# MLP chunks of a two-layer adapter network: the 256-column LoRA products placed one by one among the 512-column products

## The reference, cut to what matters

```python
def lora_add(base, inp, A, B):
    Ab = A[layer_idx][lora_indices]
    Bb = B[layer_idx][lora_indices]
    t = jnp.einsum('bri,bni->bnr', Ab, inp)
    return base + jnp.einsum('bor,bnr->bno', Bb, t) * SCALE
gate = lora_add(jnp.einsum('bnh,fh->bnf', x, W_gate), x, A_gate, B_gate)
up = lora_add(jnp.einsum('bnh,fh->bnf', x, W_up), x, A_up, B_up)
act = jax.nn.silu(gate) * up
down = lora_add(jnp.einsum('bnf,hf->bnh', act, W_down), act, A_down, B_down)
```

## Time and profile before

| | us |
|---|---|
| median of 3 runs | 700.91 (700.26 to 701.99) |
| the profiled execution's own time | 702.66 |
| its span, first to last instruction | 700.6 |
| TensorE matmul busy | 675.9 (96%) |
| VectorE, ScalarE, GpSimd busy | 313.4, 296.5, 340.0 |

### The profile page before, as it was taken

How to read it: one execution, slowest core, us unless ns; L and a number is a source line. 1 busy time by engine, 2 the same in 40 slices (tenths; PEclk the granted TensorE clock), 3 DMA queues, 4 the chain that set the end, 5 groups by cost and what they waited for, 6 DMA issues and landing times. The chain is left out here.

```text
span 700.6 us, 11139 instructions
## 1 busy us (share of the span) xinstructions
PE 675.9 (96%) x3353; PEld 561.6 (80%) x3353; DVE 313.4 (45%) x739; ACT 296.5 (42%) x642; POOL 340.0 (49%) x262
## 2 busy tenths in 40 slices
PE   4799989999999999999999999999999999999997
PEld 3578778887788888888888888888888888887775
DVE  3788567746521223731222562142373124234664
ACT  2776543334643343653333464343365343344210
POOL 0034400141787666487766578776648867400000
PEclk9999999999999999999999999999999999999999
DMA  8973561031354336254335245433424524200112
GB/s 322 349 265 136 196 225 61 15 98 47 109 165 145 111 114 240 79 168 155 111 109 172 63 142 167 138 112 120 155 80 154 166 85 137 85 0 1 61 67 113
DMA packets 32210, 91.80 MB, mean 131 GB/s; under 512 B 5312, under 2 KB 5440, under 8 KB 30624
## 3 DMA queue, kind: packets, MB, share of 16 engines
q1 hardware_dynamic: 21936, 61.05, 25.9%
q0 software_dynamic: 10080, 30.16, 12.9%
q10 hardware_dynamic: 144, 0.00, 0.0%
HBM read 81.23 MB, written 9.96 MB: 130 GB/s over the span
## 5 line engine op out<-in xcount | busy, mean ns | idle before, releaser
L570 POOL TENSOR_TENSOR gu_lo<-gu_raw,gu_hi 128x1024 fp32r<-128x1024 f32 x44 | 113.7, 2584 | 101.2 <-ACT gu_hi L646 100.2
L1263 DVE TENSOR_TENSOR act_f<-psU,silu 128x512 f32<-128x512 f32 x44 | 30.4, 692 | 187.7 <-ACT silu L819 95.8
L601 POOL DMA_INDIRECT ab<-in_ab,idx_tab x88 | 86.6, 984 | 20.7 <-issue 16.2
L819 ACT ACTIVATE silu<-psG 128x512 f32<-128x512 f32 x44 | 26.2, 597 | 153.0 <-issue 89.1
L1380 PE MATMUL psD<-act_hi,dn_hi 128*128 128x512 f32 x176 | 69.0, 392 | 0.0
L1381 PE MATMUL psD<-act_lo,dn_hi 128*128 128x512 f32 x176 | 69.0, 392 | 0.0
L1382 PE MATMUL psD<-act_hi,dn_lo 128*128 128x512 f32 x176 | 68.6, 390 | 0.0
L570 POOL TENSOR_TENSOR dn_lo<-dn_raw,dn_hi 128x512 fp32r<-128x512 f32 x44 | 57.3, 1303 | 21.0 <-ACT dn_hi L646 20.9
L575 POOL DMA_INDIRECT h_scratch<-h,idx_s x22 | 23.7, 1077 | 64.1 <-ACT h L675 32.7
L1380 PE MATMUL psG<-x_hi,gu_hi 128*128 128x512 f32 x132 | 54.2, 411 | 0.6 <-ACT silu L819 0.6
L1382 PE MATMUL psG<-x_hi,gu_lo 128*128 128x512 f32 x132 | 51.7, 392 | 0.0
(11 more groups left out here) (346 smaller groups left out, 1706.4 us busy)
## 6 DMA issues: line engine op xcount, KB each, us to landing
gu_raw<-in_gu SPq DMA_DIRECT2D x44, 512.0 KB
dn_raw<-in_dn SPq DMA_DIRECT2D x44, 256.0 KB
cond_w_raw<-in_cond_w SPq DMA_DIRECT2D x8, 1024.0 KB, 7.3
x_all<-in_x_t SPq DMA_DIRECT2D x4, 1024.0 KB, 10.7
tok<-h_scratch SPq DMA_DIRECT2D x4, 1024.0 KB, 5.5
out_t<-x_all SPq DMA_DIRECT2D x16, 256.0 KB, 2.1
ab<-in_ab,idx_tab POOLq DMA_INDIRECT x88
kraw<-in_kern SPq DMA_DIRECT2D x1, 1024.0 KB, 12.2
```

The costliest lines, as they stand in the source:

```text
L570: pool.tensor_tensor(dst, x, hi, ALU.subtract).then_inc(s, 1)
L601: pool.indirect_dma_start(ab[:, par, g, :], None, a["ab"], bass.IndirectOffsetOnAxis(idx_tab[:, NGT * t + g, fc:fc + 1], 0)).then_inc(S[f" ...
L819: act.activation(silu[:], psG[:], ACT.Silu).then_inc(S["silu_s"], 1)
L1263: dve.tensor_tensor(act_f[:], psU[:], silu[:], ALU.mult).then_inc(S["act_f_s"], 1)
```

## The change

In every step but a block's first, the eight rank products of gate and up no longer follow up as one run: one stands behind each of the first eight products of up (the four into psG first, then the four into psU). `gate_ps` is raised by the fourth, so earlier; `up_ps` by the last product of up. The wait for `bu_lo_s` moves ahead of up. In every `down` but a block's closing one, the four products into psT stand behind each of the first four into psD, and the wait for `dn_lo_s` is ahead of all of them. The first step of a block and the closing `down` keep their order. No matmul is added or taken out.

```diff
@@ down @@
-                    for g in range(NGT):
+
+                    def rank_product(i):
+                        g, x = i // 2, (act_hi, act_lo)[i % 2]
                         cols = slice(g * GT, g * GT + GT)
-                        mm = stacked(psT[:, cols], ad[:, par, g * P:g * P + P], act_hi[:, par, cols],
-                                     act_lo[:, par, cols], opens and g == 0, closes)
-                    mm.then_inc(S["td_ps"], 1)
+                        mm = pe.matmul(psT[:, cols], ad[:, par, g * P:g * P + P], x[:, par, cols],
+                                       start=opens and i == 0, stop=closes and i % 2 == 1, skip_group_check=True)
+                        if i == 3:
+                            mm.then_inc(S["td_ps"], 1)
+
+                    if closes:
+                        for i in range(4):
+                            rank_product(i)
                     pe.wait_ge(S["dn_lo_s"], n)
                     for o in range(C):
-                        mm = product(psD[:, o, :], both(dn_hi, dn_lo, al, par, slice(o * P, o * P + P)),
-                                     both(act_hi, act_lo, al, par, al), opens, False)
+                        for i, (w, x) in enumerate(((dn_hi, act_hi), (dn_hi, act_lo), (dn_lo, act_hi))):
+                            mm = pe.matmul(psD[:, o, :], w[:, par, o * P:o * P + P], x[:, par, :],
+                                           start=opens and i == 0, stop=False, skip_group_check=True)
+                            if 3 * o + i < 4 and not closes:
+                                rank_product(3 * o + i)
                     mm.then_inc(S["dn_ps"], 1)
@@ step @@
                     def gate_or_up(k, ps):
+                        xh, xl = X1[t]
                         for c in range(C):
                             at = k * D + c * P
-                            product(ps[:], both(gu_hi, gu_lo, al, par, slice(at, at + P)),
-                                    both(*X1[t], al, c, al), c == 0, False)
+                            for i, (w, x) in enumerate(((gu_hi, xh), (gu_hi, xl), (gu_lo, xh))):
+                                mm = pe.matmul(ps[:], w[:, par, at:at + P], x[:, c, :],
+                                               start=c == 0 and i == 0, stop=False, skip_group_check=True)
+                                if k == 1 and not first and 3 * c + i < 8:
+                                    rank_product(3 * c + i)
+                        return mm
+
+                    def rank_product(i):
+                        k, g, x = i // 4, i // 2 % 2, (tg_hi, tg_lo)[i % 2]
+                        cols = slice(g * GT, g * GT + GT)
+                        mm = pe.matmul((psG, psU)[k][:, cols], bu[:, par, g, k * P:k * P + P], x[:, k, cols],
+                                       start=False, stop=i % 2 == 1, skip_group_check=True)
+                        if i == 3:
+                            mm.then_inc(S["gate_ps"], 1)
+                        if i == 7 and first:
+                            mm.then_inc(S["up_ps"], 1)
...
-                    gate_or_up(1, psU)
                     if first:
+                        gate_or_up(1, psU)
                         pe.wait_ge(S["tg_lo_s"], 2 * t + 2)
-                    pe.wait_ge(S["bu_lo_s"], n + 1)
-                    for k, (ps, s) in enumerate(((psG, "gate_ps"), (psU, "up_ps"))):
-                        for g in range(NGT):
-                            cols = slice(g * GT, g * GT + GT)
-                            mm = stacked(ps[:, cols], bu[:, par, g, k * P:k * P + P], tg_hi[:, k, cols],
-                                         tg_lo[:, k, cols], False, True)
-                        mm.then_inc(S[s], 1)
+                        pe.wait_ge(S["bu_lo_s"], n + 1)
+                        for i in range(8):
+                            rank_product(i)
+                    else:
+                        pe.wait_ge(S["bu_lo_s"], n + 1)
+                        gate_or_up(1, psU).then_inc(S["up_ps"], 1)
```

## The result

The changed kernel takes 705.64 us (703.77 to 707.06, six runs) against 701.88 for the kernel before in the same comparison (six runs); the ratio is 1.0055, 95% interval 1.0036 to 1.0074. It is slower by 3.8 us where 1.2 was forecast, 0.4 above the upper end of the range. The profiled execution took 705.91 us, with a span of 703.9.

What follows compares the result with a forecast made beforehand. PE, busy 96% of the span, was taken as the bound, through start-to-start distances of matmuls. Terms 0 + 0.8 + 0.4 + 0 + 0 = +1.2 us on the median 700.91 gave 702.1 us, range 696.8 to 705.2.

Steps and rivals of the forecast that it cites:

- the first term: Twelve short products mixed among up and down: a 512 and a 256 sum to 0.3467 in any order, so 0.
- the second: Slow 512s behind a run's end: two such ends a step instead of one, 0.020 more in 40 steps, +0.8 us.
- The wait for bu_lo: Moved ahead of up: free in loop steps, 0.1 in the second step of each of four blocks, +0.4 us.
- The wait for dn_lo: Moved ahead by four short products, 0.48 us, in down; POOL makes dn_lo in the step before, so cost 0.
- The waits for at_lo between blocks: With the earlier gate_ps, three waits shrink by at most 0.19 each, -0.6 us; the gain was taken as 0.
- Rival 2: The alternation never settles, so each 512 in the mix costs more than 0.233; beyond +2.1 us given 0.23.
- its mild form: 0.005 extra on each of 19 long products in the mixes and behind: +0.075 a step, 704.3 us with bu_lo.
- its strong one: 0.009 extra on each of 19 long products in the mixes and behind: +0.15 a step, 707.3 us; outside the range.
- the change of sign: Extra on each of 19 long products in the mixes and behind from which the sign is decided, put at 0.004.
- the forecast's limit: About 0.3% (2.1 us), 0.053 us in each of 40 steps, that a measurement can tell from no change; chance within 0.46.
- The fixed part of 0.0133: Time each matmul takes beside its columns at 2.4 GHz, half of it showing up one product later.
- Rival 1: Isolated short products hide the weight load, cost 0.1133 and leave no settling: -0.10 a step, 697.3 us; chance 0.30 with shades.

Runs made afterwards that it cites:

- first and third lists of test products: Test products replacing 13 warm-up products ahead of the second layer: mixed widths, then weight columns set apart; 512,256 pairs take 0.3525 and (full loads) 0.352 us.
- The second list: Test products replacing the warm-up, with 128 or 64 weight columns, in rows of one width and mixes; 512,256 pairs with 64 take 0.343 us on the mean.

## Why the prediction was wrong

**The step that failed** is the first term and, with it, the second: the pair of a 512 and a 256 was put at 0.3467 in any order, and only one more settling of 0.020 was charged. A pair in the mix costs 0.353 (the mixed part of the step, and the first and third lists of test products), and the disturbance is not cut short but lasts through both mixes and the 512s behind them. The sum of the two terms was +0.020 a step; they measured +0.100, of which 0.085 lies in up and 0.015 in down.

**What was right.** What bounds the kernel, that only the distances between matmuls count, and that the settling belongs to the end of a run and not to its length: a single 256 leaves as much behind as twelve, and two more ends cost 0.017 each. The wait for bu_lo cost 0.3 us in four steps (0.4 forecast), by the slow product behind the wait and not by a late start. The wait for dn_lo cost nothing. Silu starts 2.0 us behind the start of up instead of 3.4, 1.4 sooner and not 1.8, since ScalarE is busy with dn_hi until then; no PE wait for it changed. The waits for at_lo between blocks fell by 0.6 us, the most that the prediction had allowed; from a block's eleventh gate to the next block's first it is 19.14, 19.05 and 19.14 us and was 19.15, 19.07 and 19.16, so they took up what these eleventh steps lost.

**What was wrong in the reasoning.** Rival 2 was what happened, between its mild form (+0.075 a step) and its strong one (+0.15). It had 0.23, and the range ended just above the mild form. In that rival's own terms, an extra on each of 19 long products, the measured +0.100 is 0.006 on each; the same terms put the change of sign at 0.001, and not at 0.004, which is where it passes the 0.053 of the forecast's limit. The fixed part of 0.0133 described the settled rows well (320 columns with full loads take 0.147 as it says), but it was read as a constant of a matmul, from which any order follows. The second list shows that it is none: with 64 weight columns it is 0.007 for 256 columns and 0.016 for 512. The rows behind the run gave a warning that was read past. The prediction says that after two long distances "the 0.227 is back"; the trace has 0.233, 0.236, 0.228, 0.233 and 0.231, so the third was only one value of a settling that lasts five, and an order that changes width with every product never lets it end. Nor does the formula of the Trainium skill that the prediction quotes (TensorE: Matmul & The Clock Gate, section "Back-to-back issue gap") support "in any order": the section gives it for an isolated product and does not speak of order, and by it 512 columns take 0.216 where this trace shows 0.227.

The likely reason for the 512 and 256 pairs, not shown to the end, is the weight load: a load takes about the 0.112 of a 128 that is bound by it, a 256 gives it 0.107 of columns, and pairs whose loads are halved settle at 0.340. The pairs of 512 and 480 do not fit it. Rival 1 suspected the load too, with the wrong sign, since it took a 512 beside a 256 to be shelter for the load. The load beside the short product is its successor's, and that is a full load in the mix as well. The 0.113 of a run's first product, which spoke for it, is only the part that is paid one product later.

Open are what PE does inside in the unsettled state and why a settling takes sometimes five products and sometimes ten; the period of three pairs is the same in the kernel and in the test rows, so it is not made by the kernel's three-part products.

## What to carry to other kernels

On a saturated PE whose matmuls each have a load of 128 weight columns, keep matmuls of one width together: a run of short ones costs its settling once at its end, mixing them one by one keeps every neighbour slow. With loads of 64 columns the pairs showed no such cost. Read a distance for a sequence only from a place where the same sequence stands; where none does, a row of test products in a spare corner of the kernel gives it in one run. Count the other lone short products too, here the transposes, and put them into the run that is there anyway; that was worth 0.17% here.

## What the runs showed of the hardware

All at the 2.4 GHz level, start to start, with operands rounded to fp32r. With 128 weight columns: 512 columns 0.227 settled, 320 0.147, 256 0.120, 128 0.112. With 64: 512 0.229, 256 0.114, 128 0.060. A 512 and a 256 in turn: 0.353 with full loads, 0.347 with the 256's halved, 0.340 with the 512's or both halved. Behind one 256, a row of them or a row of 320s, five 512s take about 0.027 more together; behind a row of 384s nine take 0.04 more, and behind a row of twelve pairs one takes 0.010 more. I had not expected that half of the weight columns makes short products faster and that the order of widths matters at all.
